# Attention in one core: pair sums folded four deep, searches at a constant rate, and a row of maxima turned on TensorE

## The reference

```python
qkv = (h @ Wqkv.T + bqkv).reshape(B, N, num_heads, hd, 3)
energy = jnp.einsum('bhqd,bhkd->bhqk', q, k)
att = jax.nn.softmax(energy, axis=-1) / D ** 0.5
out = jnp.einsum('bhqk,bhkd->bhqd', att, v)
```

## Time and profile before

| | us |
|---|---|
| median of 3 runs (3407.71 to 3416.18) | 3407.81 |
| profiled execution, its own time | 3406.56 |
| its span from first to last instruction | 3404.4 |
| attention stage in it: first score to the last multiply (L1679) | 1435.3 to 3245.6 |

### The profile page before, as it was taken

How to read it: one execution, slowest core, us unless ns; L and a number is a source line. 1 busy time by engine, 2 the same in 40 slices (tenths; PEclk the granted TensorE clock), 3 DMA queues, 4 the chain that set the end, 5 groups by cost and what they waited for, 6 DMA issues and landing times. The chain is left out here.

```text
span 3404.4 us, 41870 instructions
## 1 busy us (share of the span) xinstructions
PE 3105.9 (91%) x15302; PEld 1943.9 (57%) x15302; DVE 2211.4 (65%) x3513; ACT 1541.6 (45%) x2770; POOL 1673.7 (49%) x666
## 2 busy tenths in 40 slices
PE   4786999999997998899999999999999999999866
PEld 2675777877775777654444444444444444444355
DVE  7985222222223436478888888888888878888359
ACT  2222232232222222266666566666666656666622
POOL 2665210011111111077777677777777767777745
PEclk8887999999998999999999999999999999999978
DMA  6223100000002454465465644566444664544454
GB/s 242 86 104 125 50 13 12 25 25 25 25 13 74 169 172 155 135 149 109 87 129 126 130 87 99 106 130 136 100 87 101 141 143 87 107 87 86 84 171 150
DMA packets 137782, 347.66 MB, mean 102 GB/s; under 512 B 13767, under 2 KB 31195, under 8 KB 120842
## 3 DMA queue, kind: packets, MB, share of 16 engines
q1 hardware_dynamic: 119180, 211.20, 20.6%
q0 software_dynamic: 18432, 134.23, 19.5%
HBM read 135.34 MB, written 75.53 MB: 62 GB/s over the span
## 5 line engine op out<-in xcount | busy, mean ns | idle before, releaser
L1709 POOL TENSOR_TENSOR pair<-probs 128x2048 f32<-128x2048 f32 x256 | 1171.3, 4575 | 525.0 <-ACT probs L1644 522.9
L1667 DVE TENSOR_REDUCE part_max<-psum 128x1 f32<-128x512 f32 x1984 | 1227.9, 682 | 269.8 <-PE psum L1534 269.1
L1644 ACT ACTIVATE probs<-psum 128x512 f32<-128x512 f32 x2048 | 1083.3, 598 | 684.8 <-PE psum L1548 683.5
L1548 PE MATMUL psum<-queries,keys 97*128 97x512 f32 x2048 | 801.2, 411 | 67.9 <-DMA queries<-neg_rows 45.7
L1534 PE MATMUL psum<-keys,queries 96*128 96x512 f32 x1984 | 838.3, 423 | 5.7 <-DMA queries<-q_parts 5.7
L1534 PEld LDWEIGHTS psum<-keys,queries 96*128 96x128 f32 x1984 | 377.9, 190 | 467.2 <-DVE part_max L1667 373.6
L1559 PE MATMUL psum<-probs,values 128*32 128x512 f32 x4096 | 556.7, 616 | 2.4 <-issue 0.5
L1548 PEld LDWEIGHTS psum<-queries,keys 97*128 97x128 f32 x2048 | 384.6, 192 | 274.5 <-ACT probs L1644 151.4
L980 DVE TENSOR_TENSOR h_lo<-w_stage,h_hi 128x512 fp32r<-128x512 f32 x128 | 94.8, 740 | 529.2 <-ACT h_hi L918 529.2
L911 ACT ACTIVATE w_stage<-psum,b_col 128x512 f32<-128x512 f32 x128 | 88.1, 689 | 509.4 <-PE psum L38 509.4
L1024 POOL TENSOR_TENSOR ffn_u_lo<-ffn_u,ffn_u_hi 128x512 fp32r<-128x512 f32 x32 | 41.2, 1286 | 553.7 <-DVE ffn_u_hi L970 553.7
(11 more groups left out here) (306 smaller groups left out, 3754.8 us busy)
## 6 DMA issues: line engine op xcount, KB each, us to landing
pair<-pair POOLq DMA_DIRECT2D x128, 1024.0 KB, 7.2
queries<-q_parts SPq DMA_DIRECT2D x96, 256.0 KB, 4.8
keys<-k_parts SPq DMA_DIRECT2D x42, 512.0 KB, 7.3
x<-in_x_dram SPq DMA_DIRECT2D x8, 1024.0 KB, 7.3
y<-in_x_dram SPq DMA_DIRECT2D x8, 1024.0 KB, 5.6
y_rows<-y SPq DMA_DIRECT2D x8, 1024.0 KB, 5.1
qkv_z<-z_rows SPq DMA_DIRECT2D x8, 1024.0 KB, 5.8
q_parts<-qk_hi SPq DMA_DIRECT2D x32, 256.0 KB, 2.1
```

The lines of the kernel that those rows point to most:

```text
L1548: nc.tensor.matmul(psum[:, SC + unit % 3, :], keys[n // PB][0:R + 1, h, kt * P:(kt + 1) * P], queries[n][0:R + 1, h, :], start=True, stop= ...
L1644: act.activation(probs[tile % NPROB][:, h, :], psum[:, SC + unit % 3, :], ACT.Exp).then_inc(exp_ready, 1)
L1667: dve.tensor_reduce(part_max[:, at, kc:kc + 1], psum[:, MX + j % 3, :], AX.X, ALU.max).then_inc(max_read, 1)
L1709: pool.tensor_tensor(pair[number % NPAIR][:, :, :], probs[2 * number % NPROB][:, :, :], probs[(2 * number + 1) % NPROB][:, :, :], ALU.add) ...
```

## The change

- **Folds.** Four pair buffers are folded in a chain instead of two: buffer 0 onto 1, 1 onto 2, 2 onto 3. That is six folds and two bursts of ones in a block, where there were four and four. Each fold still waits for all earlier ones. `SUM_LAG` goes from 9 to 14 tiles.
- **Searches.** `SHARES` goes; a formula gives 5 searches to each of the first 20 tiles and 4 to every later one, 20 searches ahead of the block's own pace. The last 21 tiles have none.
- **Row of maxima.** VectorE reduces the maxima, TensorE transposes them (`turn`, at tile 12 of the block before) into a ring slot, VectorE negates from there (`negate`), and one transfer brings 16 rows of 128 to the queries, in place of four transfers.
- **Denominators.** Each row of 512 denominators stands 32 times over. VectorE turns the tile by a 32 by 32 transpose, inverts 16 columns instead of 512, and spreads them by a second transpose (tiles 8, 9 and 10). The ones become sqrt(512), which takes over the scaling. The final multiply moves to GpSimd, ahead of its sixth add of a block.
- **Buffers.** 3 query buffers instead of 4; loops written out with plain numbers.

```diff
@@ -1391,49 +1391,66 @@
     R = 3 * HD
     NKT = L // P
     NKC = L // CH
-    PB = 2
-    NB = PB * B
-    PER_GROUP = B * NCH // NB
-    ITERS = NG * PER_GROUP
+    BLOCKS = NG * B * NCH
     PAIRS = NKT // 2
-    NPROB, NPAIR = 6, 4
-    QUADS = PAIRS // 2
+    FOLDED = 4
+    SUMS = PAIRS // FOLDED
+    NPROB, NPAIR, NQ = 6, 4, 3
     MAXES = HG * TT * NKC
-    SHARES = [4] + [5] * 12 + [0] * 3
-    AV_LAG, SUM_LAG = 2, 9
-    Q_LD, ROW_LD = 3 * 16, 4 * 16
+    UNITS = HG * NKT
+    AV_LAG, SUM_LAG = 2, 14
+    RATE, AHEAD, TURN_KT = 4, 20, 12
+    FIRST_TURN = 14
...
+    rows = sb("att_rows", [HG * TT, P], F32R)
     o_sum, den, att = sb("o_sum", [P, CH]), sb("den", [P, CH]), sb("att", [P, CH])
+    inv = sb("den_inverse", [P, CH // HD])
...
+    def searched(tile):
+        return min((RATE + 1) * tile, RATE * tile + AHEAD, MAXES * (BLOCKS - 1))
+    def turn_of(tile):
+        if tile == FIRST_TURN:
+            return 1
+        if tile % NKT == TURN_KT and 1 < tile // NKT + 1 < BLOCKS:
+            return tile // NKT + 1
+        return None
...
-            def load_max_row(count, n):
-                sp.wait_ge(neg_ready, count + 1)
-                load_max_rows(sp, queries[n], neg_rows, q_ld[n])
+            def load_max_row(count):
+                sp.wait_ge(neg_ready, count)
+                row = queries[count % NQ][R:R + 1, :, :].bitcast(F32).rearrange("o h (t i) -> o (h t) i", i=P)
+                sp.dma_start(row, rows[:, :].bitcast(F32)).then_inc(row_ld, 16)
...
+            for count in range(BLOCKS):
+                b, chunk = place(count)
+                g = group(count)
+                ends = chunk == NCH - 1 and g < NG - 1
+                if ends:
+                    sp.wait_ge(sc_ready, UNITS * count + UNITS // 2)
+                    load_keys(g + 1, b, 0)
+                if count < BLOCKS - 1:
+                    load_max_row(count + 1)
+                sp.wait_ge(sc_ready, UNITS * (count + 1))
+                if ends:
+                    load_keys(g + 1, b, 1)
+                if count + NQ < BLOCKS:
+                    load_queries(count + NQ)
+                if ends:
+                    sp.wait_ge(av_ready, NKT * (count + 1))
+                    load_values(g + 1, b)
+                if count > 0:
+                    store(count - 1)
...
+            def turn(count):
+                pe.wait_ge(max_final, count)
+                nc.tensor.transpose(ring_slot()[0:HG * TT, 0:P], maxima[:, 0:HG * TT], ident[:, :]).then_inc(max_ready, 1)
...
+            def total(part):
+                count, r = part // SUMS, part % SUMS
+                pe.wait_ge(folded, 16 * (FOLDED - 1) * (part + 1))
...
                 mm.then_inc(sums_ready, 1)
...
-                    share = [next(j, None) for _ in range(SHARES[kt])]
...
-                    score(it, n, kt, 0)
-                    searches()
-                    score(it, n, kt, 1)
-                    searches()
-                    if kt >= AV_LAG or not first:
-                        weigh(*lagged(it, n, kt, AV_LAG))
-                    if (kt - SUM_LAG) % 4 == 0 and (kt >= SUM_LAG or not first):
-                        total(*quad_of(*lagged(it, n, kt, SUM_LAG)))
-                    searches()
-                    score(it, n, kt, 2)
-                    searches()
-                    score(it, n, kt, 3)
-                    searches()
...
+            for tile in range(BLOCKS * NKT):
+                count, kt = tile // NKT, tile % NKT
+                found = range(searched(tile), searched(tile + 1))
+                if turn_of(tile) is not None:
+                    turn(turn_of(tile))
+                if tile == AV_LAG:
+                    pe.wait_ge(consts, 1)
+                    pe.wait_ge(ones_ld, 16 * (B - 1))
+                for h in range(HG):
+                    score(count, kt, h)
+                    for s in found[h:h + 1]:
+                        search(s)
+                    if h == 1:
+                        if tile >= AV_LAG:
+                            weigh(tile - AV_LAG)
+                        if tile >= SUM_LAG and (tile - SUM_LAG) % (2 * FOLDED) == 0:
+                            total((tile - SUM_LAG) // (2 * FOLDED))
+                        for s in found[HG:]:
+                            search(s)
...
-            def finish(count):
-                dve.wait_ge(max_read, MAXES * (count + 1))
-                negate_maxima(dve, first, turning, 2 * (count - 1), neg_ready)
+            def negate(count):
+                if count > 1:
+                    dve.wait_ge(row_ld, 16 * (count - 1))
+                dve.tensor_scalar(rows[:, :], ring_slot()[0:HG * TT, 0:P], -1.0, None, ALU.mult).then_inc(neg_ready, 1)
+                dve.wait_ge(neg_ready, count)
+                dve.sem_inc(max_read, 1)
...
-            def normalise(count):
...
-                dve.reciprocal(den[:, :], den[:, :]).then_inc(inverted, 1)
...
-                dve.scalar_tensor_tensor(out=att[:, :], in0=o_sum[:, :], scalar=float(D) ** -0.5, in1=den[:, :],
-                                         op0=ALU.mult, op1=ALU.mult).then_inc(att_ready, 1)
...
+            def turn_sums(count):
                 dve.wait_ge(den_copied, count + 2)
+                dve.wait_ge(att_st, 16 * (count + 1))
+                dve.transpose(att[:, :], den[:, :]).then_inc(den_turned, 1)
+            def invert(count):
+                dve.wait_ge(den_turned, count + 1)
+                dve.reciprocal(inv[:, :], att[:, :].rearrange("p (c j) -> p c j", j=HD)[:, :, 0]).then_inc(inverted, 1)
+            def spread_inverse(count):
                 dve.wait_ge(inverted, count + 1)
+                dve.transpose(den[:, :].rearrange("p (c j) -> p c j", j=HD),
+                              inv[:, :].unsqueeze(2).broadcast_to((P, CH // HD, HD))).then_inc(spread, 1)
+            for tile in range(BLOCKS * NKT):
+                count, kt = tile // NKT, tile % NKT
+                if turn_of(tile) is not None:
+                    negate(turn_of(tile))
+                for s in range(searched(tile), searched(tile + 1)):
+                    find(s)
+                if count > 0 and kt == 8:
+                    turn_sums(count - 1)
+                if count > 0 and kt == 9:
+                    invert(count - 1)
+                if count > 0 and kt == 10:
+                    spread_inverse(count - 1)
...
-            def one(it, n, first, last):
-                count = NB * it + n
-                for p in range(PAIRS):
-                    number = PAIRS * count + p
-                    pool.wait_ge(exp_ready, 2 * HG * (number + 1))
-                    quad = QUADS * count + p // 2
...
-                    if p % 2 == 1:
-                        pool.wait_ge(pair_ready, number + 1)
-                        if quad > 0:
-                            pool.wait_ge(folded, 16 * quad)
-                        pool.dma_start(pair[number % NPAIR][:, :, :], pair[(number - 1) % NPAIR][:, :, :],
-                                       accum_op=ALU.add).then_inc(folded, 16)
+            def normalise(count):
+                pool.wait_ge(spread, count + 1)
+                pool.wait_ge(o_copied, count + 2)
+                pool.tensor_tensor(att[:, :], o_sum[:, :], den[:, :], ALU.mult).then_inc(att_ready, 1)
+            for number in range(PAIRS * BLOCKS):
+                count, p = number // PAIRS, number % PAIRS
+                part, member = number // FOLDED, number % FOLDED
+                folds = (FOLDED - 1) * part + max(member - 1, 0)
+                if p == 5 and count > 0:
+                    normalise(count - 1)
+                pool.wait_ge(exp_ready, 2 * HG * (number + 1))
+                if number >= NPAIR:
+                    if member < FOLDED - 1:
+                        pool.wait_ge(folded, 16 * ((FOLDED - 1) * (part - 1) + member + 1))
+                    else:
+                        pool.wait_ge(sums_ready, part)
+                pool.tensor_tensor(pair[number % NPAIR][:, :, :], probs[2 * number % NPROB][:, :, :],
+                                   probs[(2 * number + 1) % NPROB][:, :, :], ALU.add).then_inc(pair_ready, 1)
+                if member > 0:
+                    pool.wait_ge(pair_ready, number + 1)
+                    if folds > 0:
+                        pool.wait_ge(folded, 16 * folds)
+                    pool.dma_start(pair[number % NPAIR][:, :, :], pair[(number - 1) % NPAIR][:, :, :],
+                                   accum_op=ALU.add).then_inc(folded, 16)
+            normalise(BLOCKS - 1)
```

More of the change, by code:

```diff
@@ L1517, in _ @@
-            for g in range(NG):
-                group(g, g == 0, g == NG - 1)
-            store(B * NCH * NG - 1, NG - 1, B - 1, NCH - 1)
-            sp.wait_ge(att_st, 16 * (B * NCH * NG + 1))
+            for count in range(BLOCKS):
+                b, chunk = place(count)
+                g = group(count)
+                ends = chunk == NCH - 1 and g < NG - 1
```

(60 more changed lines are left out.)

194 lines of the change are left out of this document (66 added, 128 removed).

## The result

The changed kernel takes **3457.47 us** (median of 4 runs, 3453.97 to 3458.88); the kernel before, on the same chip, 3408.76. The ratio is 1.0137, with a 95% interval of 1.0119 to 1.0154: slower by 1.4%, 49 us. The prediction had 3398. The profiled execution took 3456.15, its span is 3454.4.

The account below looks back on a forecast made before the run. GpSimd's queue of folds was to bound the kernel: parts 1573, multiplies 43, late folds 8, meetings 54 and 95 make 1773 us from first add to last fold, giving 3398 as a median; range 3315 to 3485.

Parts of the forecast that it names:

- 128 steps from a landing to the next issue: GpSimd's folds: second waits for first, third for second; 7.0 each alone, 7.05 with the step between.
- last fold to next first fold: GpSimd between parts of four pairs: issue, two adds and gaps, 10.5 us; a final multiply adds 1.4.
- late landings of folds that are waited for: Folds delayed by loads: 8 us for the first two, 54 in plain blocks, 95 in key blocks.
- first add to first fold: Start of GpSimd's chain: first part counted without the first issue and gap, put at 9.5 us.
- Undisturbed blocks: Attention block without delayed folds: TensorE 51.3 us, GpSimd 50.6, so nearly equal.
- Meetings: Folds meeting loads in the DMA queues: 2.3 us in each of 23 plain blocks, 15.8 in each of 6 key blocks.
- The rule on the queues: DMA engines taking turns between queues: said to disagree with the earlier trace, zero fold packets in 4.6 us.
- an order of arrival: DMA queues: a fold waits for all that was ahead of it, and what comes later waits for the fold.
- rival B: DMA queues: folds and loads share packet by packet, 46 + 55 replaces 149 us, time 3350; chance 0.14.
- A: Attention stage: folds not disturbed as placed, TensorE stays the bound, time 3255; chance 0.16.
- C: VectorE's transposes wait for GpSimd's adds, two waits of up to 4.6 us a block, time 3495; chance 0.09.
- The multiply on GpSimd: Final multiply between two GpSimd adds, where nothing hides it: 1.4 us each, 43 for 31.

Follow-up runs that it names:

- the tree: Changed kernel, six folds without a chain, five pair buffers, multiply one pair later, bursts of ones two tiles later, weights loaded behind the folds: 3314.67 us, ratio 0.9723.
- the experiment: Changed kernel with only the final multiply moved from ahead of GpSimd's sixth add of a block to ahead of the seventh: 3421.28 us, ratio 1.0032.
- the tree with spread loads: Unchained six-fold version with second half of keys loaded a quarter into the next block and values in its middle: 3311.23 us, ratio 0.9710.

## Why the prediction was wrong

The forecast for the stretch from the first add to the last fold was 1773; it took 1828 (1451.2 to 3279.4). By its own terms, over the 64 parts:

| term | put | measured | difference |
|---|---|---|---|
| 128 steps from a landing to the next issue | 0.05 each, 6 | 0.55 each, 71 | +64 |
| last fold to next first fold, 63, multiplies in them | 706 | 691 | -15 |
| late landings of folds that are waited for | 8 + 54 + 95 = 157 | 159 | +2 |
| first add to first fold | 9.5 | 11.9 | +2 |

The step that failed is "7.0 each when alone, 7.05 with the step between": the step is 0.55, not 0.05. In the kernel before no fold was ready and waiting for a landing, so its trace did not show the step, and I gave no bounds for it although the text did so for smaller gaps. TensorE's matmuls do start 0.04 after a landing in that trace (31 waits for the row of maxima, L1548); for an issue by GpSimd the nearest row was another, and at hand: a fold waits 0.30 for an add that has just ended. With 0.30 for the step the sum would have been 3430; with the measured 0.55 it gives 3462, against 3457. The median of 0.54 is the same within 0.01 in all seven kernels with chains (means of 0.55), so it belongs to the wait and not to a meeting.

The trace also tells on which side of the wait the half microsecond lies. GpSimd's instruction that waits for the landing (L1736), ahead of the fold issued at 2975.30:

```profile
L1736 POOLq EVENT_SEMAPHORE  x1: 17/17/17, 2974.8 to 2974.8; - x1
```

The fold of 2967.82 lands 6.9 later, at 2974.8, and the wait's record starts there, 0.02 behind the landing, as at the other folds. So the landing is seen at once, and the 0.5 passes between the end of the wait and the issue. What GpSimd does in it is not shown, and no run changed this step alone.

The 15 that came back stand in the intervals between parts: undisturbed they are 10.27 where 10.5 was put, since an add starts 0.25 before the record of the issue ahead of it ends (2957.55 + 0.86 and 2958.16), and the multiply is 1.26, not 1.4.

**Undisturbed blocks.** TensorE 51.4 (put 51.3). GpSimd 51.7 (put 50.6), so the two were not "nearly equal, 51.3 and 50.6": the order was reversed, and TensorE could not win back in plain blocks what key blocks had lost.

**Meetings.** 2.3 was put on a plain block, 2.9 measured; 15.8 on a key block, 14.2 measured. Over all blocks that is 10 too little and 10 too much, and they cancel: that the sum was right to 2 us is luck in part. I had the plain fold ahead of the queries untouched and the next paying 2.3; in the rows above the first paid 2.4 and the next 1.1.

**The rule on the queues.** The Trainium skill (DMA: Bandwidth & Descriptors, section SWDGE vs HWDGE vs iDMA) has each engine take turns between its queues. The prediction said that the trace of before does not agree, and read an order of arrival out of its shares. The numbers of packets say more. Queues before, 1785 to 1789, and after, 2070.5 to 2073.5, while a fold and loads both move:

```profile
q0 software_dynamic: 100, 0.82, 98.1%
q1 hardware_dynamic: 99, 0.05, 6.3%
...
q0 software_dynamic: 64, 0.52, 84.2%
q1 hardware_dynamic: 64, 0.13, 13.1%
```

The two queues move the same number of packets, 100 and 99, 64 and 64: they do take turns, and the skill's rule agrees there. The fold gets most of the time because its packets are 8 KB and the others' 0.5 to 2 KB. What the rule does not give is how long a fold stands before its first packet: 4.6 us without one in the earlier trace rows, beside 452 of q1. Such waits are a large part of the late landings, and rival B, which let a fold be held by 8 packets only, had 101 us for plain and key blocks; 149 were measured.

**Rivals.** A, TensorE as the bound, fell by the waits. Its time of 3255 is not reached even by the tree, whose blocks mostly do take 51.3; late folds with the slow clock behind them are 24 us of the 60 between (3 blocks of 8); the rest was not taken apart. C, transposes held by GpSimd's adds, fell too:

```profile
L1682 DVE STREAM_TRANSPOSE att<-den x32: 699/701/711, 1529.3 to 3289.0; 128x512 f32<-128x512 f32 x32
...
L1690 DVE STREAM_TRANSPOSE den<-den_inverse x32: 699/701/711, 1535.7 to 3290.0; 128x512 f32<-128x512 f32 x32
```

Every transpose took the 0.7 that was put, with none above 0.711, where the old multiply with two inputs took 691 ns at the least and 3981 at the median. The page "SBUF — State Buffer" of the Trainium skill (section Who interferes with whom), by which a VectorE instruction with at most one SBUF input, outside the 2-port modes, does not contend with GpSimd, agrees with this. The multiply on GpSimd was put at 1.4 and cost 1.26 beyond its neighbours (11.54 - 10.27), and 36 us in all by the experiment.

**The direction** then follows. All edits but the chain gain 83 us (3409 to 3326), and the chain takes 132. The forecast did have the folds as the bound and gave them 144 of TensorE's 153 us, which left a gain of 9. The 59 by which it missed are the 64 of that one term and some 9 of small ones (2 and 2 in the table, 2 by which the first add came later, 3 behind the last fold), less the 15 of the intervals. So the mechanism, a chain of folds that disturbances lengthen, was right, and one term of its sum was mis-sized.

## What to carry to other kernels

When a change makes instructions wait for one another's transfers, price the step from landing to issue from the nearest wait in the trace, and multiply it by its count, before pricing anything rarer: half a microsecond at 128 places outweighed every meeting that was mis-sized. Taking slack away from a queue turns all its old, free delays into time, so count those too; the trace of before gave them to within 10 us for each kind of block. And which of six transfers waits for which can be worth some 107 us, the chain with the multiply moved against the tree: make independent ones first, and let the dependent one go behind the next piece of work.

## What was not expected of the hardware

- From a fold's landing to the issue of the one that waits for it 0.54 us pass (median of 128 places in the changed kernel; 0.53 to 1.9), more than the 0.30 from the end of an add to an issue, though the wait itself ends 0.02 after the landing.
- A wait of TensorE of about 5 us is followed by a stretch at half the granted clock: 0.50, or 1.2 GHz, from 1892 to 1898 in the tree with spread loads, after 1.00 until the wait. In the tree a wait of 5 us cost 8.
- A transfer issued 0.4 us after a fold, on another queue, can still move part of its packets ahead of it. Once both queues move they take turns packet by packet (64 and 64, 100 and 99), so the one with 8 KB packets gets 84 to 98% of the engines' time.
